# Stores moved into a convolution, and two row products of TensorE drawn apart

## What is computed

```
def reference(x, w_real, w_imag, b_real, b_imag, W, weight):
    # group norm, then a complex 3 x 3 convolution of the spectrum, with biases, and back
    x = x + irfftn(conv(rfftn(gn(x)), w_real + 1j * w_imag) + b)
    # a gate for each row of the image: keep it or not, by the sign of a product with column sums
    x = x + gates(gn(x)) * gn(x)
    x = x + conv3x3(gn(x), W)
    x = x + conv3x3(gn(x), weight)
    return x
```

## Time and profile before

| | |
|---|---|
| runs, median of 3 | 4691.74 us (4676.85 to 4695.56) |
| profiled execution | 4709.38 us, its span 4707.6 us |
| PE busy | 4279.1 us (91%) |
| DVE busy | 3334.5 us (71%) |
| ACT busy | 2540.4 us (54%) |
| moved by DMA | 468.06 MB, 99 GB/s on the mean |

### The profile page before, as it was taken

How to read it: one execution, slowest core, us unless ns; L and a number is a source line. 1 busy time by engine, 2 the same in 40 slices (tenths; PEclk the granted TensorE clock), 3 DMA queues, 4 the chain that set the end, 5 groups by cost and what they waited for, 6 DMA issues and landing times.

```text
span 4707.6 us, 229463 instructions
## 1 busy us (share of the span) xinstructions
PE 4279.1 (91%) x85024; PEld 2675.9 (57%) x85024; DVE 3334.5 (71%) x13348; ACT 2540.4 (54%) x8637; POOL 1.0 (0%) x6
## 2 busy tenths in 40 slices
PE   4999988999999998999989999899998999988898
PEld 1455765556655566555655566555665557655476
DVE  2887757876578765887658875688756887578863
ACT  4675526655266543666436654366633666345562
POOL 0000000000000000000000000000000000000000
PEclk8999999999999999999999999999999999999999
DMA  7442015620155202651035510356003650034204
GB/s 190 130 136 76 4 40 171 189 89 4 49 185 182 74 3 62 187 186 54 3 85 183 183 38 3 94 181 187 27 3 108 186 181 14 3 109 139 88 4 146
DMA packets 290246, 468.06 MB, mean 99 GB/s; under 512 B 25536, under 2 KB 92288, under 8 KB 289408
## 3 DMA queue, kind: packets, MB, share of 16 engines
q1 hardware_dynamic: 289536, 457.92, 32.4%
HBM read 323.60 MB, written 134.22 MB: 97 GB/s over the span
## 4 chain that ended last, share of the span: by engine, by line
PE 60%; DVE 12%; DMA 8%; issue 8%; SPq 5%; ACT 3%; DVEq 1%; ACTq 1%
PE ps L1361 34%; PE ps L1255 9%; DMA raw<-x 8%; PE ps L1270 5%; PE ps L1263 3%; PE ps L1279 3%; PE ps L1125 2%; DVE shared L858 2%; SPq L426 2%; SPq L433 2%; DVE xin L853 1%; DVE shared L854 1%; SPq L407 1%; ACT x L584 1%; DVE xin L852 1%
## 5 line engine op out<-in xcount | busy, mean ns | idle before, releaser
L1361 PE MATMUL ps<-x,conv_s 32*32 32x512 f32 x49104 | 1741.9, 606 | 62.4 <-DVE x L1087 30.0
L1361 PEld LDWEIGHTS ps<-x,conv_s 32*32 32x32 f32 x49104 | 1242.5, 104 | 509.5 <-issue 273.7
L1255 PE MATMUL ps<-shared 32*32 32x512 f32 x16384 | 657.4, 604 | 0.0
L1270 PEld LDWEIGHTS ps<-hil,shared 128*128 128x128 f32 x4096 | 504.6, 194 | 194.0 <-issue 193.2
L662 ACT ACTIVATE x<-ps,vec 128x256 f32<-128x256 f32 x512 | 214.6, 470 | 741.4 <-PE ps L1361 741.4
L584 ACT ACTIVATE x<-ps,vec 128x128 f32 (+1 forms) x1024 | 377.6, 385 | 432.2 <-PE ps L1270 431.2
L858 DVE SCALAR_TENSOR_TENSOR shared<-xin,trig 128x128 f32<-128x128 f32 x2048 | 533.8, 301 | 106.7 <-DVE shared L854 98.8
L1279 PE MATMUL ps<-eye,vsb 128*128 128x128 f32 x2048 | 370.7, 305 | 237.1 <-DVE vsb L879 134.1
L1270 PE MATMUL ps<-hil,shared 128*128 128x128 f32 x4096 | 572.5, 284 | 0.0
L1086 DVE SCALAR_TENSOR_TENSOR x<-ps,x 128x256 f32<-128x256 f32 x512 | 214.8, 420 | 427.2 <-ACT x L662 426.2
L1255 PEld LDWEIGHTS ps<-shared 32*32 32x32 f32 x16384 | 310.3, 104 | 278.8 <-issue 213.2
(11 more groups left out here) (204 smaller groups left out, 4711.7 us busy)
## 6 DMA issues: line engine op xcount, KB each, us to landing
out<-x SPq DMA_DIRECT2D x512, 256.0 KB
shared<-x SPq DMA_DIRECT2D x448, 256.0 KB
raw<-x SPq DMA_DIRECT2D x256, 256.0 KB
raw<-x SPq DMA_DIRECT2D x512, 128.0 KB
shared<-t_strip SPq DMA_DIRECT2D x512, 96.0 KB, 4.0
x<-x SPq DMA_DIRECT2D x64, 256.0 KB, 8.8
x<-t_proj SPq DMA_DIRECT2D x1, 2048.0 KB, 11.8
trig<-t_trig SPq DMA_DIRECT2D x1, 512.0 KB, 12.1
```

The lines of the kernel that those rows point to most:

```text
L1255: mm = pe.matmul(ps[TM * cg:TM * cg + TM, bank, :], wst[TM * rg:TM * rg + TM, k, v, a, :], of[TM * rg:TM * rg + TM, :], start=(a == AXS), ...
L1270: mm = pe.matmul(quarter(ps[:, BY + 2 * odd + e, :], int(q < 2), q % 2), xt[:, e, q, :], hil[:, q, 0:P], start=False, stop=True, skip_grou ...
L1361: mm = pe.matmul(halves(ps[TM * cg:TM * cg + TM, banks[k], :]), conv_s[TM * rg:TM * rg + TM, kw, second, :], x1b[TM * rg:TM * rg + TM, of, ...
```

## The change

- **SP:** an image's strips 0 to 55 are stored during its own third convolution, in loops of four, and 8 (DEFERRED) in the next image's first layer. The loads of the next image's first three pairs stand between these stores: pair 0, strips to 36, pair 1, strips to 48, pair 2, strips to 56. Before, pair 2 was loaded when the next image began.
- **PE:** add_u takes one strip; in a step the order is mix, even row term, even Hilbert product, even turn, odd row term, odd Hilbert product, odd turn, projection. The wait for the eviction of Y's banks, before one for the pair ahead of the mix, is now one for each strip, ahead of the strip's first products.
- **Turn:** the identity has 32 more columns, and the transposes use it from column 32, so that BX holds its rows as xt wants them; ACT copies it in one operation.
- **ACT:** the even copy from BX comes ahead of both evictions.
- **DVE:** in make_planes the difference is made ahead of the sum, and two waits that stood right behind the operation waited for are looser. The planes of pairs 0 and 1 are made after pairs 17 and 23.

```diff
-DEFERRED = STRIPS - 2 * UNROLL
+DEFERRED = 2 * UNROLL
+STORED_BY = (36, 48, STRIPS - DEFERRED)
-U_AT, C_AT, PLANES_AT = (5, 8), (12, 14, 16), (20, 22)
+U_AT, C_AT, PLANES_AT = (5, 8), (12, 14, 16), (17, 23)
...
-        "t_eye": f(np.eye(P)), ...
+        "t_eye": f(np.arange(P + TM) % P == p[:, None]), ...
...
-            for pair in range(2):
+            for pair in range(AHEAD):
                 load_pair(0, pair, 2 * pair)
...
-                for pair in range(2, AHEAD):
-                    load_pair(i, pair, 2 * pair)
-                for pair in range(DEFERRED // 2):
+                for pair in range(PAIRS):
                     feed(pair, 2 * pair % TABLES)
-                    if stores_left:
+                    if stores_left and pair < DEFERRED // 2:
                         for e in range(2):
-                            store(i - 1, STRIPS - DEFERRED + pair * 2 + e)
-                for pair in range(PAIRS - UNROLL, PAIRS):
-                    feed(pair, 2 * pair % TABLES)
+                            s = STRIPS - DEFERRED + pair * 2 + e
+                            store(i - 1, s, s % STORE_SEMS, s // STORE_SEMS)
+
+                def stores(first, last):
+
+                    with sp.Fori(first // STORE_SEMS, last // STORE_SEMS) as j:
+                        for k in range(STORE_SEMS):
+                            store(i, j * STORE_SEMS + k, k, j)
+
                 if more:
-                    for pair in range(2):
+                    stored = 0
+                    for pair, until in enumerate(STORED_BY):
                         load_pair(i + 1, pair, 2 * pair)
-
-                for n in range(PAIRS):
-                    if more and n >= PAIRS - (STRIPS - DEFERRED):
-                        sp.wait_ge(evicted, ev(i, 1 + STRIPS + 2 * n + 2))
-                        sp.sem_inc(s_sp, 1)
-                        store(i, n - (PAIRS - (STRIPS - DEFERRED)))
-                    elif not more:
-                        for e in range(2):
-                            store(i, 2 * n + e)
+                        stores(stored, until)
+                        stored = until
+                else:
+                    stores(0, STRIPS)
...
-                    nc.scalar.activation(xt[:, e, :, 0:P - TM], flipped[:, :, TM:P], ACT.Identity)
-                    nc.scalar.activation(xt[:, e, :, P - TM:P], flipped[:, :, 0:TM], ACT.Identity).then_inc(xt_ready, 1)
+                    nc.scalar.activation(xt[:, e], flipped, ACT.Identity).then_inc(xt_ready, 1)
...
                     copy_v(t)
+                    turned_out(t * 2, 0)
                     for e in range(2):
                         evict(t * 2 - 2 + e, e, BY + 2 * (1 - odd) + e, 2 * (1 - odd) + e, uses)
-                        turned_out(t * 2 + e, e)
+                    turned_out(t * 2 + 1, 1)
                     squares(t * 2 - 2, 2 * (1 - odd), uses)
...
-                    b.did(V.scalar_tensor_tensor(plus, raw[:, e, 0:HALF], v1(MEAN2), raw[:, e, HALF:N], ALU.subtract, ALU.add))
-                    V.tensor_tensor(minus, raw[:, e, 0:HALF], raw[:, e, HALF:N], ALU.subtract).then_inc(x_taken, 1)
-                    b.then(V.scalar_tensor_tensor(fg(wst[:, k]), fg(mix_s[:, 1]), row_trig[:, 0, bass.ds(s, 1)], fg(mix_s[:, 0]), ALU.mult, ALU.add))
-                    dve.wait_ge(x_taken, i * STRIPS + s + 1 + RAW)
+                    b.did(V.tensor_tensor(minus, raw[:, e, 0:HALF], raw[:, e, HALF:N], ALU.subtract))
+                    V.scalar_tensor_tensor(plus, raw[:, e, 0:HALF], v1(MEAN2), raw[:, e, HALF:N], ALU.subtract, ALU.add).then_inc(x_taken, 1)
+                    b.did(V.scalar_tensor_tensor(fg(wst[:, k]), fg(mix_s[:, 1]), row_trig[:, 0, bass.ds(s, 1)], fg(mix_s[:, 0]), ALU.mult, ALU.add))
+                    b.settle(but=1)
...
-                    pe.wait_ge(y_evicted, t0 + t * 2 - 2) if type(t) is not int or t > 1 else None
-                    due()
...
                     for a in (AXS, AXB, AXC):
                         for e in range(2):
+                            if a == AXS and (type(t) is not int or t > 1):
+                                pe.wait_ge(y_evicted, t0 + t * 2 - 3 + e)
+                                due()
...
-                        mm = pe.transpose(ps[:, BX, q * P:(q + 1) * P], chunk(q)(vsb[:, e, :]), eye[:])
+                        mm = pe.transpose(ps[:, BX, q * P:(q + 1) * P], chunk(q)(vsb[:, e, :]), eye[:, TM:TM + P])
...
                     mix(t, odd)
-                    add_u(t - 1, 1 - odd, table, table_uses)
                     for e in range(2):
+                        add_u(e, 1 - odd, table, table_uses)
                         hilbert(t * 2 - 2 + e, e, 1 - odd)
                         turn(t, e)
                     project_next(2 * (1 - odd), table, uses, first)
```

More of the change, by code:

```diff
@@ L143, in tables @@
     return {
-        "t_eye": f(np.eye(P)), "t_hil": f(hil_t), "t_fix": f(mean_fix), "t_trig": f(trig_cols),
+        "t_eye": f(np.arange(P + TM) % P == p[:, None]), "t_hil": f(hil_t), "t_fix": f(mean_fix), "t_trig": f(trig_cols),
         "t_strip": f(strip), "t_rows": f(row_trig), "t_gsel": f(gsel), "t_gnext": f(gsel_next), "t_proj": f(strip[:, :, P:].transpose(1, 0, 2).reshape(P, STRIPS * HP)), "t_zsel": f(zsel), "t_fold": f(fold), "t_ends": f(ends), "t_partner": f(partner),
@@ L223, in program @@
         BTAIL = 7
-        eye = sb("eye", P, P)
+        eye = sb("eye", P, P + TM)
         hil = sb("hil", P, 4, HW_)
@@ L417, in _, with store @@
                 sp.sem_inc(c_stored[k], STORES)
-            def store(i, s):
-                k = s % STORE_SEMS
+            def store(i, s, k, turn):
                 sp.wait_ge(evicted, ev(i, 1 + STRIPS + s + 1))
                 sp.sem_inc(s_sp, 1)
-                sp.wait_ge(c_stored[k], (i + 1) * STORES + s // STORE_SEMS * 16)
+                sp.wait_ge(c_stored[k], (i + 1) * STORES + turn * 16)
                 sp.sem_inc(s_sp, 1)
-                sp.dma_start(out[i].rearrange("c (s r) w -> s r c w", r=ROWS)[s], x1[:, s, 0:N]).then_inc(c_stored[k], 16)
+                sp.dma_start(out[i].rearrange("c (s r) w -> s r c w", r=ROWS)[s], x1[:, bass.ds(s, 1), 0:N]).then_inc(c_stored[k], 16)
             def load_next(image, s, t, k):
@@ L859, in make_planes @@
                                                          ALU.mult, ALU.mult, accum_out=gsum[:, 2 * a + q, bass.ds(s, 1)]))
+                        if a == 0:
+                            dve.wait_ge(x_taken, i * STRIPS + s + 1 + RAW)
                         ins = V.tensor_tensor(planes[:, a, k, HALF:N], plus, trig[:, a, 0:HALF], ALU.mult)
@@ L862, in make_planes @@
                             b.did(ins)
+                            b.settle(but=3)
                             b.did(V.scalar_tensor_tensor(fg(wst[:, k]), fg(mix_s[:, 2]), row_trig[:, 1, bass.ds(s, 1)], fg(wst[:, k]), ALU.mult, ALU.add))
@@ L1257, in mix, with add_u @@
                     mm.then_inc(mixed, 1)
-                def add_u(t, odd, table, uses):
-                    for e in range(2):
-                        pe.wait_ge(tab_loaded[table + e], (i * (STRIPS // TABLES) + uses + 1) * 16)
-                        pe.matmul(ps[:, BY + 2 * odd + e, :], strip[HP * e:HP * e + HP, table + e, 0:P], u[HP * e:HP * e + HP, :],
-                                  start=False, stop=False, skip_group_check=True)
+                def add_u(e, odd, table, uses):
+                    pe.wait_ge(tab_loaded[table + e], (i * (STRIPS // TABLES) + uses + 1) * 16)
+                    pe.matmul(ps[:, BY + 2 * odd + e, :], strip[HP * e:HP * e + HP, table + e, 0:P], u[HP * e:HP * e + HP, :],
+                              start=False, stop=False, skip_group_check=True)
                 def hilbert(s, e, odd):
@@ L1312, in first_layer @@
                     step(t, t % 2, (t - 1) // 2, 2 * (t - 1) % TABLES, STRIPS // TABLES - 1)
-                add_u(PAIRS - 1, 1, TABLES - 2, STRIPS // TABLES - 1)
                 for e in range(2):
+                    add_u(e, 1, TABLES - 2, STRIPS // TABLES - 1)
                     hilbert(STRIPS - 2 + e, e, 1)
@@ L1332, in keep_clock @@
                 for _ in range(count):
-                    pe.matmul(ps[:, BY + 2, :], eye[:], trig[:, 0, :], start=True, stop=True)
+                    pe.matmul(ps[:, BY + 2, :], eye[:, 0:P], trig[:, 0, :], start=True, stop=True)
             def first_statistics(i, more):
```

## The result

The median of eight runs of the changed kernel is 4742.02 us (4730.79 to 4750.05); the kernel before, run beside it eight times, took 4696.67 us (4676.85 to 4716.73). The ratio is 1.0092, 95% interval 1.0071 to 1.0112: 45 us slower, where 90 were forecast. The profiled execution took 4730.8 us (span 4729.0), that of before 4709.4. What follows is read stage by stage.

The account below looks back on a forecast made before the run. PE was taken to set the pace. First layers +15, +6, +4, ends +9, turn of the loop -12, third convolution +47 and +21 sum to +90 us on 4691.7: 4782 us, range 4665 to 4840.

Parts of the forecast that it names:

- The step: First layer, PE: one step of a pair of strips goes from 9.22 us in image 0 to 9.69.
- The lone row term: First layer, PE: a row term standing alone ahead of the odd product costs the whole pair's 1.06 us, not 0.53.
- the wait in the mix: First layer, PE's wait on the evicted strip, now inside the mix: taken as 0.1 us a step, up to 0.63.
- First layers: First layers, before the turn of the loop: image 0 +15 us, images 1 to 6 +6 together, image 7 +4.
- the turn of the loop: Start of the next image: stores end four pairs earlier, code and data come sooner; 0 to -5 us each, -12 taken.
- Tails: End of each first layer: the lone term stands ahead of the edge terms DVE waits for, 1.1 x 8 = +9 us.
- Third convolution: Third convolution with 56 stores an image: code late behind stores +47 us, planes' two separate bursts +21 us.
- DVE's second stop: Third convolution: planes made six pairs apart stop PE twice, not once; +3 us an image, +21 in all.
- The late work behind stores: Third convolution: PE's code arrives late behind stores, 0.31 us a pair over 28 pairs; +47 us, range 0 to +70.
- a sign that I had named: Third convolution: 150 GB/s or more, PE idle without a cause some 5 us in each, two stops for DVE.
- Rival 2: Third convolution: code keeps up with the stores, each block on the chip in time; 4735 us, chance 0.18.
- rival 4: Worse: code late in all 28 pairs +23, low clock after bursts +17, no gain at loop's turn +12; 4834 us, chance 0.08.
- Rival 1: First layer: the lone row term is short, 0.53 us, and fills ACT's delay; 4649 us, chance 0.12.

Follow-up runs that it names:

- The short stores: Changed kernel with each store writing only the first 64 of a strip's 512 columns, as many stores and waits as before: 4699.98 us, ratio 1.0001.
- the kernel with both terms together: Changed kernel with a step's two row terms back to back again, ahead of both Hilbert products, all else as changed: 4545.06 us, ratio 0.968.

## Why the prediction was right in kind and twice too large

**The step.** 9.69 was forecast and 9.66 is measured. The lone row term costs the whole pair, as taken: 1.05. The Trainium skill (TensorE: Matmul & The Clock Gate, "Why this matters for your kernels") has a small product take the time of a full one; this case now shows it for 64 of 128 rows (1.05, where a product on the whole array takes 0.98). The two sides of that sum were less exact than their total. The step without waits was put at 8.33 and is 8.68 (mix 3.48, not 3.33; second product 1.03, not 0.89; the last switch 0.64, not 0.57), and the lone term was put at 1.36 with its switches and the wait in the mix, and costs 0.98. The errors of 0.35 and 0.38 cancelled, which is luck.

**First layers.** Image 0: +15 forecast, +13 measured. Image 7: +4, and +8 (its step was put at 9.28 and is 9.47). Images 1 to 6: -6 forecast with the turn of the loop, and -33 measured. Here the turn was mis-sized: I took 2 us of a bound of 5. The first step fell from 12.5 to 7.8 on the mean, almost the whole bound, and the 6 us that I left in as DVE's late start at the turn were mostly these same microseconds. Quiet queues at the turn, which I gave as the reason, are the smaller part of it: with SP's old queue in the changed kernel the first step is down to 9.0 already. The larger part came with the other edits, to which I gave nothing at the turn; which one stays open.

**Tails.** +9 forecast for the lone term ahead of the edge terms. From the last mix to the first eviction of the third convolution it takes 157.5 us in images 0 to 6, before and after; the last image fell from 156.2 to 152.3. This step failed; no run isolates why the term doesn't show there.

**Third convolution.** +68 forecast, +37 measured. DVE's second stop: 3 us an image taken, 2.9 measured with the short stores. The late work behind stores: 7 an image taken (47 in all), 2.7 measured (19 in all). The direction is as forecast, the size is not, and a sign that I had named failed: of the 5 us of idle time without a cause in each convolution and the 150 GB/s, image 1 shows 1.6 and 139. I carried image 7's 0.31 us a pair over to the other images. The short stores show that image 7 loses some 10 us by the bytes, 0.3 a pair, and that images 0 to 6 lose a quarter of it. These run at 3.9 us a pair, with DVE's stops in between and 139 GB/s in place of 155; that this slack is what hides the rest wasn't tested. Rival 2 had this cost at nothing, and the Trainium skill (Runtime: NRT & Kernel Launch, "Instruction fetch mechanics") calls the fetch of code mostly hidden: in images 0 to 6 that is nearer to the rows than my term, in image 7 it is not.

**The sum.** Three terms carry 68 of the 69 us between the +90 and the +21 of the two profiles: 28 in the late work, 27 in the layers of images 1 to 6, 13 in the tails; the small ones nearly cancel. (In rival 4 the forecast has +23 for code late in all 28 pairs; by its own price of 8.7 an image, less the 2 that it takes off, this is 12, and that rival 4823.) The medians differ by 45; one execution of each kernel doesn't tell which stages the other 24 belong to. Rival 1 (a short lone term) is ruled out by 1.05 us. What I had not priced is the other side of the change: without the split it would have gained 152 us. I gave ACT's new order no gain of its own, since PE's longer step hid it; that order alone ends the delay that the split was to fill.

## What to carry to other kernels

Two products on half of the array's rows that share their time are worth keeping together: parting them to fill a stall costs a whole product each, so look first for what ends the stall on the other engine. Price the parts of a change apart: here a gain of 152 us and a loss of 197 came in one diff. The split was to fill a stall that another edit of the same diff had ended, and its longer step hid most of what the move of the stores brings (49 us are left of 133). Stores moved out of one stage arrive in another, and what they delay there can be small waits at the turn of a loop as well as loads.

## What the runs showed of the hardware

A short stall can cost PE more than its length. In the kernel with both terms together, image 4, DVE's copy comes 1.99 us late, and the products behind the wait are slow (timeline of PE):

```profile
2405.89 0.74 PE L1282 MATMUL ps<-eye,vsb 128*128 128x128 f32 x4 [1.99 <-DVE vsb L882]
2406.47 1.57 PE L1273 MATMUL ps<-hil,shared 128*128 128x128 f32 x8
...
2408.82 1.77 PE L1128 MATMUL ps<-shared 128*64 128x512 f32 x4
```

The product that takes 1.06 in a flat step takes 1.57, and the projection 1.77 in place of 1.08, and the granted clock, at its higher level (2.4 GHz) in the step before, falls below it for a part of this one (windows as above; 0.87 is the mean):

```profile
2389.00:2398.00 9.00, 9.00 (x132) 5.26 (x128) 5.17 (x21) 6.63 (x24) 0.00 (x0) 1.00 0.65 187
2398.00:2410.00 12.00, 10.01 (x130) 5.96 (x128) 10.98 (x50) 7.23 (x24) 0.00 (x0) 0.87 0.61 174
```

The step became 12.43 us long, 3.7 more than 8.69, for a wait of 2.0.

An engine that waits for no one can be late, too: DVE was idle 7.42, 5.77 and 4.51 us at the turn into image 1 in runs whose stores went on up to it, and only waited for PE, 2.33, where they had ended 8.5 us before. It was 3.16 in the changed kernel with SP's queue as before, where they went on as well, so the stores alone don't set the length.
